# Three subtractions per expert moved from GpSimd to VectorE in a fused attention and mixture-of-experts kernel

## What is computed

```python
x = x + attention(layernorm(x))   # 16 heads of 16, scores kept only for |i - j| <= half (at most 60)
x = x + experts(layernorm(x))     # 8 experts, the top 2 of a softmax gate per token
# experts(X): gate = softmax(X @ Wg + bg); for the two best experts e of each token:
#   h = silu((X @ W1[e] + b1[e]) * (X @ W3[e] + b3[e]))
#   mixed = sum over the two of gate * (h @ W2[e] + b2[e]);  result = mixed @ Wf + bf
```

## Time and profile before

| | |
|---|---|
| median of 3 runs | 1354.57 us (1354.25 to 1356.06) |
| profiled execution | 1353.25 us, of which the span from first to last instruction is 1351.5 us |
| PE busy | 1175.3 us (87% of the span) |
| DVE busy | 970.8 us (72%) |
| ACT busy | 782.4 us (58%) |
| POOL busy | 605.6 us (45%) |
| 24 low halves on POOL (L754) | 54.0 us, 2280 ns each on average |

### The profile page before, as it was taken

One profiled execution on the slowest core, in us unless ns is written; L12 is line 12 of the kernel. 1 busy time (PEld: TensorE's weight loads), 2 busy tenths in 40 slices (PEclk: granted clock), 3 DMA queues, 4 the chain that ended last, 5 costly groups with the idle time before them and its releaser, 6 DMA issues. The chain is left out here.

```text
span 1351.5 us, 47132 instructions
## 1 busy us (share of the span) xinstructions
PE 1175.3 (87%) x18161; PEld 869.7 (64%) x18177; DVE 970.8 (72%) x2167; ACT 782.4 (58%) x1463; POOL 605.6 (45%) x648
## 2 busy tenths in 40 slices
PE   4798898888888889888888259999999999999996
PEld 2464555555555545555454148888888888888885
DVE  5345868789787877878766537777777777777775
ACT  4347776776767767677565125544555445455553
POOL 2301324546545465554535715444444444454454
PEclk9899999999999989999896679999999999999999
DMA  4875554766646666465725244656645755645554
GB/s 147 242 227 115 159 149 120 210 165 188 180 111 196 166 192 175 116 183 144 213 58 176 86 135 63 110 85 125 133 57 68 176 78 71 126 65 70 64 64 48
DMA packets 211580, 177.54 MB, mean 131 GB/s; under 512 B 115522, under 2 KB 175562, under 8 KB 211290
## 3 DMA queue, kind: packets, MB, share of 16 engines
q1 hardware_dynamic: 153482, 117.78, 34.0%
q0 software_dynamic: 25728, 34.17, 15.0%
q10 hardware_dynamic: 32208, 23.33, 6.6%
HBM read 67.99 MB, written 89.90 MB: 117 GB/s over the span
## 5 line engine op out<-in xcount | busy, mean ns | idle before, releaser
L1642 PE MATMUL p_h<-xt_parts,w_hi 128*128 128x256 f16 x1824 | 273.7, 273 | 7.3 <-DVE xt_parts L1729 6.9
L1058 DVE TENSOR_REDUCE mx<-p_max 128x4 f32<-128x496 f32 (+1 forms) x248 | 211.4, 853 | 93.2 <-PE p_max L1340 92.7
L855 ACT ACTIVATE probs<-p_exp,unscale 128x736 f32<-128x736 f32 (+1 forms) x256 | 210.3, 821 | 76.1 <-PE p_exp L1340 50.3
L1788 POOL DMA_INDIRECT out<-yw,tokens x136 | 220.7, 1623 | 45.9 <-POOL tick L1787 34.7
L1733 DVE SCALAR_TENSOR_TENSOR t<-p_h,b,t 128x256 f32<-128x256 f32 x272 | 125.8, 481 | 105.3 <-ACT t L1681 99.7
L1642 PEld LDWEIGHTS p_h<-xt_parts,w_hi 128*128 128x128 f16 x1824 | 177.4, 98 | 31.3 <-DVE t L1733 9.7
L1787 POOL TENSOR_TENSOR tick<-tick 128x1 f32<-128x1 f32 x136 | 65.4, 481 | 265.4 <-ACT yw L1698 265.4
L1681 ACT ACTIVATE t<-p_h,b,undo 128x256 f32<-128x256 f32 x272 | 142.1, 554 | 67.8 <-PE p_h L1642 62.9
L1642 PE MATMUL p_h<-xt_parts,w_lo 128*128 128x256 f16 x912 | 174.0, 273 | 0.0
L744 POOL DMA_INDIRECT routed<-rows,slots x128 | 130.5, 1020 | 38.9 <-issue 38.9
L1375 PE MATMUL p_out<-probs,v 64*32 64x184 f32 (+1 forms) x4096 | 138.1, 327 | 8.3 <-DVE out_t L1071 7.7
(11 more groups left out here) (274 smaller groups left out, 2524.3 us busy)
## 6 DMA issues: line engine op xcount, KB each, us to landing
qk_dram<-qk_hi SPq DMA_DIRECT2D x128, 128.0 KB, 2.6
qs<-qk_dram SPq DMA_DIRECT2D x64, 192.0 KB, 4.3
ks<-qk_dram SPq DMA_DIRECT2D x64, 192.0 KB, 4.3
x_in<-in_x SPq DMA_DIRECT2D x64, 128.0 KB, 3.4
qk_dram<-qk_lo SPq DMA_DIRECT2D x64, 128.0 KB, 2.4
w_mat<-in_W ACTq DMA_DIRECT2D x32, 256.0 KB
out<-x_sb SPq DMA_DIRECT2D x64, 128.0 KB
w_split<-w_first_hi SPq DMA_DIRECT2D x24, 256.0 KB
```

What stands on the lines that cost most here:

```text
L855: nc.scalar.activation(probs[r % 3][:, :, 0:hi - lo].rearrange("p (e s) w -> p e s w", e=2), p_exp[:, :, 0:2 * WIN].rearrange("p e (s w) - ...
L1058: nc.vector.tensor_reduce(out=maxes, in_=max_buffer(r, p_max, p_exp)[:, :, 0:2 * WIN].rearrange("p e (s w) -> p e s w", s=2)[:, :, :, 0:hi ...
L1642: last = nc.tensor.matmul(p_h[:, m % KC, k, :], w[e][a][:, k, HID * c + P * m:HID * c + P * m + P], xt[:, x, c, :], start=(n == 0 and c == ...
L1788: nc.gpsimd.indirect_dma_start(out=io["out"].rearrange("b s d -> (b s) d"), out_offset=bass.IndirectOffsetOnAxis(ap=tokens[:, b, :].bitcas ...
```

## The change

The three subtractions of each expert are issued by DVE instead of POOL, with the same operands, and the second one is placed in round 9 instead of round 7. In DVE's list they stand after `scaled_weights` and before `logits`, `softmax_gates`, `take_out` and `divide` of the same round, and after `row_max` and `turn_back`.

```diff
-LOWW_AT = (23, 23, 27)
+LOWW_AT = (23,25,27)
@@ the gpsimd block
-            def low_weights(e, k):
-                pool.wait_ge(s_whi, 3 * e + k + 1)
-                nc.gpsimd.tensor_tensor(w_lo[:, k, :], w_mat[:, k, :], w_hi[:, k, :], ALU.subtract).then_inc(s_wlo, 1)
-
...
-                    for e, k in due_expert(LOWW_AT, i, n):
-                        low_weights(e, k)
@@ the vector block
+            def low_weights(e, k):
+                dve.wait_ge(s_whi, 3 * e + k + 1)
+                nc.vector.tensor_tensor(w_lo[:, k, :], w_mat[:, k, :], w_hi[:, k, :], ALU.subtract).then_inc(s_wlo, 1)
+
...
                     for e, k in due_expert(SCALE_AT, i, n):
                         scaled_weights(e, k)
+                    for e, k in due_expert(LOWW_AT, i, n):
+                        low_weights(e, k)
                     for b, _ in due(LG_AT, i, n):
                         logits(b)
```

## The result

The changed kernel takes 1361.19 us (median of 7 runs, 1358.02 to 1362.43), the kernel before on the same chip 1354.57 (7 runs): ratio 1.0044, 95% interval 1.0031 to 1.0057. It is slower by 4 to 8 us; 8.8 were forecast, with a range of 1356.5 to 1371.5. The profiled execution took 1358.12 us (span 1356.4), 4.9 more than the one of before.

What follows compares the result with a forecast made beforehand. DVE's list was taken to bound rounds 8 to 14 of odd steps, ACT's load wait second. Seven odd steps 11.5, step 15 0.3, tail -3.0: 8.8 us onto the median, 1363.4 us, range 1356.5 to 1371.5.

Steps and rivals of the forecast that it cites:

- the tail's gain: After step 15, POOL freed of 6.75 us of low halves catches up: 3.0 us saved, range 1 to 4.
- steps 1 and 2: Odd step 1 grows with DVE's list, less 0.4 us; even step 2 unchanged; 2.7 us forecast together.
- Rival B: Each subtraction takes only 0.75 us: about 1355 us, no change; chance 0.09.
- The division goes back to 0.69: Round 10, odd steps: without POOL's low halves beside it, step 3's division falls from 1.90 to 0.69 us.
- DVE's list sets the odd steps: Rounds 8 to 14: three subtractions add 3.45 us per odd step, less what the division gives back.
- rival E: PE's and DVE's later waits near step end absorb the delay: about 1356 us, no change; chance 0.05.
- D: Slack in rounds 8 to 10 hides the first two subtractions: 1346.6 us, faster; chance 0.06.
- the walk: Step 3 traced instruction by instruction: round 8's maximum 1.15 us later, round 12's 2.24 us, PE's round 15 2.2 us.
- The load gate: ACT's wait for the third low half before loading the next expert: 1.9 us later in step 3, second to DVE.
- step 9: Division had escaped and ACT waited 3.18 us for POOL; list grows 3.25 us, 2.4 less arrives.
- rival F: More PE waiting lowers the granted clock: 1368 to 1374 us; chance 0.06.
- Rival C: DVE's subtractions wait for POOL's scatters and norm in rounds 9 to 11: 7 us more, 1370.5 us; chance 0.12.

Runs made afterwards that it cites:

- e2_tiny: Changed kernel with each DVE subtraction cut to one of 1024 columns, so most low halves are left out: 1334.19 us, ratio 0.9853 to the kernel before.
- e1_gate: Changed kernel with ACT's loads for the next expert two rounds later: 1358.63 us, ratio 1.0026 to the kernel before.
- e4_gate_before: Kernel before with ACT's loads for the next expert two rounds later: 1347.92 us, ratio 0.9947.
- e3_last: Kernel before with only the last expert's three low halves on DVE: 1351.67 us, ratio 0.9974.
- e12_last_gate: Kernel before with the last expert's low halves on DVE and ACT's loads two rounds later: 1345.29 us, ratio 0.9944.
- e9_again: Changed kernel run again unaltered on another chip: 1357.21 us, ratio 1.0031 to the kernel before.
- e10_echo: Changed kernel plus unused POOL subtractions on constants in the old places, first seven experts: 1378.53 us, ratio 1.0179 to the kernel before.
- e11_mix: Kernel before with low halves split between POOL and DVE, the last expert's all on DVE, loads from round 15: 1353.51 us, ratio 0.9991.

## Why the prediction was right

Direction and mechanism were right, and the time lies in the range; the size was forecast too high, 8.8 us for 4 to 8 measured. It came as near as it did partly by luck, since errors of both signs cancel: by profile steps 3, 9 and 13 were forecast 1.0, 1.6 and 0.4 us too high and the tail's gain 0.7 too low, steps 1 and 2 together 1.9 too low. Steps 5, 7 and 11 were right to about 0.1. Point by point:

- **A subtraction is 1.23 us.** It is 1.208 on average over 24 (1.18 to 1.27). Rival B (0.75) is out.
- **The division goes back to 0.69.** It does, 695 ns over 32. DVE's busy time grew by 17.9 us (970.8 to 988.7); the forecast 17.3 is of the list, which counts each subtraction without its overlap of 0.08.
- **DVE's list sets the odd steps.** Shown by e2_tiny, in which 16.0 us less of DVE's time in five odd steps bring 15.9 us, and by e1_gate against e4_gate_before: 15.9 us in seven odd steps for 17.0 of DVE's time. That is also against rival E as a whole, and against D: there was no slack in rounds 8 to 10 for the first two subtractions. In step 3 PE waits 1.15 us for a row maximum before it begins round 9 at 241.51, where it had begun without a wait.
- **What did not arrive.** Of 3.45 us per odd step 3.1 do, by the table. Step 3 shows where the rest goes: 1.81 us are there at round 12 (2.24 by the walk; round 8's maximum was 0.79 later instead of 1.15), and DVE's wait for PE at the end of the step gives back 0.5 more. The prediction denied this ("these waits are for each other and shift along"): a small part of rival E is true. Against the kernel before, step by step, the six odd steps other than 9 fall short of the list's growth by 2.2 us together, nearly half of it in step 3; the prediction had taken off 0.8 in these (steps 7 and 13) and 0.4 in step 1, where nothing was to be taken off.
- **The load gate.** This is the term that was mis-sized. The prediction took 2.4 us off for step 9. By the table the gate held 4.3 us there before and next to nothing after. The step itself went from 45.5 to 44.7 where 0.8 more was forecast, and this 1.6 is the largest single error. A small gate also stood in step 3 of the kernel before: its length less division is 40.9 us, and 40.8 in e3_last, but 40.4 in e4_gate_before and in e12_last_gate, where the load is moved.
- **Steps 1 and 2** went the other way: 4.6 us together in the changed kernel's profile, with 2.7 forecast. TensorE was granted 0.92 over each there (rows above), where step 2 of before had 1.00, and step 2's PE time is 38.1 us instead of 35.5. In e9_again both came to 3.1 us, with step 1 at 1.00 and step 2 at 0.96. Steps 3 and 9 of e9_again:

```profile
216.75:261.59 44.84, 38.62 (x820) 23.43 (x821) 38.84 (x85) 30.00 (x47) 20.20 (x20) 0.92 0.65 176
470.29:514.73 44.44, 35.94 (x820) 22.25 (x821) 38.68 (x85) 29.78 (x47) 20.10 (x20) 1.00 0.61 169
```

  The first profile of the same kernel has step 3 at 1.00 and 44.1 us and step 9 at 0.92 and 44.7. In these two pairs the step at 0.92 is 0.2 and 0.8 us longer than the same step at 1.00. That the subtractions cause it, as rival F has it, is not shown: e2_tiny, nearly without them, has step 2 at 0.92 and 41.5 us too.
- **Rival C.** Not in the changed kernel: none of 24 subtractions is over 1.27 us beside scatters. It exists beside a POOL subtraction (e10_echo, 2.82 us).
- **The tail** gave 3.7 us in the profile (e9_again 3.0), forecast 3.0.

Attention 9.8 instead of 11.8 and the tail 3.7 instead of 3.0 make 6.1 instead of 8.8, and the medians say 3.3 (e9_again) to 6.6. What is left between these is setup and expert stage, which differ by one to three microseconds between executions of any two of these kernels, and stays open.

The Trainium skill, SBUF — State Buffer, section "Who interferes with whom", says that whoever issues first on the shared ports holds them for its whole instruction. The row of e10_echo (2.82 us for a subtraction that began inside POOL's) agrees. `var` of e11_mix (2.83 us) does not end before POOL's low half either, but by its row it began 0.65 us ahead of it, so the order of issue is not shown there. The runs also show how to read the rule: it works between two instructions that overlap in time, so it said nothing against this change once POOL's subtractions were gone.

## What to carry to other kernels

Before work is moved off a lightly used engine, find the list that sets the pace of the steps where it lies; here the mean load of DVE (77% of attention) hid that from round 8 to round 14 of an odd step it had no free time, and nearly every microsecond given to it was paid. Price the wait that the old place caused as well: a gain of about the size of the change's loss could be had by moving the wait (e4_gate_before), and a smaller one by giving DVE only the expert for which it had time (e3_last). A contention that was moved away from one instruction landed on the next one in the chain (e11_mix), so look at the new place too. And one profile is one phase: which step the gate held differed between two kernels with the same program there (step 9, or 7 and 11).

## What the runs showed of the hardware that was not expected

- A division that meets POOL's low halves ends at one of two instants. In the seven odd steps up to 13 of the kernel before, e3_last, e4_gate_before and e12_last_gate, 28 in all, it ends 2.7 us (six) or 4.8 us (22) after POOL's first subtraction began. The six had begun 1.5 to 2.0 us after it, the others 2.1 us or more. Step 3 and step 9 of the kernel before are one of each. So in these kernels 0.2 us in when it begins decided over 2 us.
- A scatter instruction on POOL gets longer beside DVE's subtraction: the 128 scatters went from 130.5 to 137.9 us (1020 to 1077 ns), and in step 3 of the changed kernel two that run beside a subtraction take 1.82 and 1.88 us. The same two take 0.96 and 1.04 in e2_tiny, where the subtraction is cut to one column and the 128 take 130.6 us again:

```profile
237.43 1.82 POOL L744 DMA_INDIRECT routed<-rows,slots  x1 [0.30 <-issue]
...
243.17 1.88 POOL L744 DMA_INDIRECT routed<-rows,slots  x1 [0.49 <-issue]
245.35 0.96 POOL L744 DMA_INDIRECT routed<-rows,slots  x1 [0.30 <-issue]
```

- A DVE instruction on four elements per partition can take 2.83 us instead of 0.16 when POOL subtracts 1024 elements beside it (e11_mix).
- The same program with the same waits did not always get the same clock from TensorE. In step 1 of the changed kernel PE was busy 3.77 of 6.00 us in one stretch and was granted 0.81; in the next two it had all its time filled, first at 0.62 and then at 1.00, so part of the way it ran at the lower of its two levels with work at hand:

```profile
156.00:162.00 6.00, 3.77 (x108) 2.06 (x100) 5.83 (x9) 3.95 (x7) 0.00 (x0) 0.81 0.55 167
162.00:168.00 6.00, 6.00 (x111) 3.39 (x98) 5.54 (x15) 4.16 (x7) 0.00 (x0) 0.62 0.94 181
168.00:174.71 6.71, 6.70 (x134) 3.21 (x127) 3.01 (x4) 5.51 (x10) 1.15 (x1) 1.00 0.80 258
```

  In e9_again, the same kernel, PE was busy for the same 3.77 us in that place of step 1 and kept 1.00, and the step was 0.7 us shorter:

```profile
157.83:163.83 6.00, 3.77 (x112) 2.12 (x104) 5.83 (x9) 4.55 (x8) 0.00 (x0) 1.00 0.61 180
163.83:169.83 6.00, 4.18 (x110) 2.48 (x109) 5.74 (x16) 4.20 (x8) 0.00 (x0) 1.00 0.93 262
```

- The kernel before took 1354 to 1355 us beside every run at the usual clock (0.949 to 0.966 over the span), and 1454.95 on the slower chip at 0.914 to 0.933 (7% more). There what hurt DVE counted for less: the echo's ratio was 1.0179 at the usual clock and 1.008 there. The gain of e12_last_gate went from 0.9944 to 0.9973, with intervals that overlap.
